# Twenty of the 96 pieces of the experts' weights are split in the state space stage instead of the second cross-attention

## What is computed

```python
x = x + _L0_xattn_ref(_layernorm(x), ctx_1024, ctx_1024, fside, mask, ...)   # cross-attention, 16 heads
x = x + _L0_attn_ref(_layernorm(x), ...)                                    # self-attention
x = x + _L0_ffn_ref(_layernorm(x), ...)                                     # experts, first kind
x = x + _L1_xattn_ref(_layernorm(x), ctx_1024, ...)                         # second cross-attention
x = x + _L1_attn_ref(_layernorm(x), a_params, B_w, C_w, D)                  # state space recurrence
x = x + _L1_ffn_ref(_layernorm(x), ...)                                     # attention with rotation, then top-2 of 8 experts
```

## Time and profile before

| | us |
|---|---|
| median of 3 runs | 1137.86 |
| lowest and highest | 1136.81, 1143.95 |
| profiled execution, its own time | 1140.91 |
| its span (first to last instruction) | 1139.1 |
| PE busy | 839.9 (74%) |
| DVE busy | 586.6 (51%) |
| ACT busy | 447.3 (39%) |
| POOL busy | 398.5 (35%) |
| mean granted clock of TensorE | 0.853 of full |

### The profile page before, as it was taken

The page is one execution under the profiler, slowest core; times in us unless marked ns, Lnnn a source line. Parts: engine busy times, 40 slices in busy tenths (PEclk is TensorE's granted clock), DMA queues, the critical chain, the costliest instruction groups (busy, mean ns, idle before and its releaser), DMA issues.

```text
span 1139.1 us, 23921 instructions
## 1 busy us (share of the span) xinstructions
PE 839.9 (74%) x8324; PEld 662.2 (58%) x8324; DVE 586.6 (51%) x1548; ACT 447.3 (39%) x1619; POOL 398.5 (35%) x577
## 2 busy tenths in 40 slices
PE   2898898689798768888876625675548887788880
PEld 1666666578653346666654514563438786787770
DVE  2477777568644335664563765764314443334342
ACT  1565666356523216655651023664003232222220
POOL 3455655535477742443345323224340000000005
PEclk9999999889889779999995657876559988888885
DMA  7111114523224523243324002111197788886754
GB/s 307 47 47 55 39 53 133 210 76 109 92 99 148 171 98 103 92 139 120 109 77 145 0 1 93 39 38 48 62 328 282 282 291 309 298 301 244 263 211 115
DMA packets 90181, 161.62 MB, mean 142 GB/s; under 512 B 9840, under 2 KB 23920, under 8 KB 89328
## 3 DMA queue, kind: packets, MB, share of 16 engines
q1 hardware_dynamic: 88560, 156.30, 40.1%
q0 software_dynamic: 1536, 4.20, 1.2%
HBM read 126.13 MB, written 34.34 MB: 141 GB/s over the span
## 4 chain that ended last, share of the span: by engine, by line
PE 36%; DMA 15%; DVE 14%; ACT 14%; POOL 9%; issue 9%; SPq 1%; DVEq 0%; POOLq 0%; ACTq 0%
DMA kbuf<-in_b 10%; ACT probs L1094 5%; PE ps L491 4%; PE ps L493 4%; PE ps L492 4%; PE ps L528 3%; ACT probs L1053 3%; PE ps L571 3%; PE ps L587 2%; DMA ctx_t<-in_ctx 2%; PE ps L540 2%; DVE stat L1439 2%; ACT probs L1044 2%; PE ps L620 1%; ACT pt L1033 1%
## 5 line engine op out<-in xcount | busy, mean ns | idle before, releaser
L491 PE MATMUL ps<-qbuf,arena 128*128 128x128 f16 x736 | 149.1, 241 | 46.3 <-DMA kbuf<-in_b 45.7
L492 PE MATMUL ps<-qbuf,arena 128*128 128x128 f16 x736 | 148.9, 241 | 0.0
L493 PE MATMUL ps<-qbuf,arena 128*128 128x128 f16 x736 | 148.4, 240 | 0.0
L1902 DVE SCALAR_TENSOR_TENSOR probs<-ps,kbuf,ctx_t 128x128 f32<-128x128 f32 x184 | 51.8, 344 | 168.9 <-ACT ctx_t L1206 168.9
L1259 POOL TENSOR_TENSOR piece_out<-piece_in,piece_out 128x512 f16<-128x512 f32 x96 | 113.8, 1185 | 7.7
L1422 POOL DMA_INDIRECT pt<-y_rows,neg x16 | 15.4, 960 | 276.0 <-DMA y_rows<-vbuf 271.5
L1206 ACT ACTIVATE ctx_t<-ps,kbuf 128x128 f32<-128x128 f32 x184 | 52.6, 369 | 150.0 <-PE ps L493 150.0
L1227 POOL TENSOR_TENSOR var<-mv,half 128x1 f32<-128x1 f32 x56 | 11.2, 199 | 283.1 <-DVE mv L1440 196.3
L491 PEld LDWEIGHTS ps<-qbuf,arena 128*128 128x128 f16 x736 | 81.0, 110 | 48.6 <-DMA kbuf<-in_b 47.6
L1284 POOL TENSOR_TENSOR probs<-probs,gp 128x512 f32<-128x512 f32 x64 | 81.3, 1302 | 52.4 <-ACT probs L1044 52.4
L571 PE MATMUL ps<-pack_const,probs 128*128 128x128 f32 x512 | 76.5, 285 | 28.8 <-DVE vbuf L1481 11.2
(11 more groups left out here) (231 smaller groups left out, 2003.6 us busy)
## 6 DMA issues: line engine op xcount, KB each, us to landing
arena<-w_parts SPq DMA_DIRECT2D x23, 3072.0 KB, 11.1
piece_in<-in_w SPq DMA_DIRECT2D x96, 256.0 KB, 2.8
w_parts<-piece_out SPq DMA_DIRECT2D x96, 256.0 KB, 2.1
ctx_t<-in_ctx SPq DMA_DIRECT2D x32, 256.0 KB, 2.7
x_rows<-piece_out SPq DMA_DIRECT2D x1, 2944.0 KB, 16.5
qbuf<-x_rows SPq DMA_DIRECT2D x23, 128.0 KB, 9.9
y_rows<-vbuf SPq DMA_DIRECT2D x23, 128.0 KB, 9.7
arena<-in_xa SPq DMA_DIRECT2D x2, 1282.0 KB, 7.0
```

What stands on the lines that cost most here:

```text
L491: pe.matmul(dst, a[0], b[0], start=first, stop=False)
L492: pe.matmul(dst, a[0], b[1], start=False, stop=False)
L493: return pe.matmul(dst, a[1], b[0], start=False, stop=final)
```

## The change

In "xa1" each of the 20 steps splits one piece instead of two, and SyncE passes one piece ahead of each context load. In "ssm" each of the ten steps splits two pieces at its end. The number of splits up to "la" stays 82, and SyncE's loop over the remaining pieces begins earlier.

```diff
         XA1_PIECES = 2 * INNER_STEPS + 2 * (TILES + 1)
-        LA_PIECES = XA1_PIECES + 2 * (SEQS + 4)
+        LA_PIECES = XA1_PIECES + SEQS + 4 + 2 * (TILES + 2)
...
             for k in range(SEQS + 4):
-                pass_piece(XA1_PIECES + 2 * k)
-                pass_piece(XA1_PIECES + 2 * k + 1)
+                pass_piece(XA1_PIECES + k)
                 if k + 2 < SEQS:
                     load_context("xa1", k + 2, k % 2)
-            for c in range(LA_PIECES, EXPERTS * PIECES):
+            for c in range(XA1_PIECES + SEQS + 4, EXPERTS * PIECES):
                 pass_piece(c)
...
                     if st == "xa1":
-                        for j in range(2):
-                            split_piece(j, k + XA1_PIECES // 2)
+                        split_piece(s, h + XA1_PIECES // 2)
                     chain.restart()
...
                     if live(k, 2, TILES):
                         root_of_variance(g, k - 2)
+                    for j in range(2):
+                        split_piece(j, k + (XA1_PIECES + SEQS + 4) // 2)
                     chain.restart()
                 skewed(pool, TILES, 2, ssm_step)
```

## The result

The changed kernel takes 1144.91 us (median of 20 runs, 1141.12 to 1149.09) against 1139.16 (20 runs, 1134.47 to 1146.62) for the kernel before: a ratio of 1.0043 with a 95% interval of 1.0027 to 1.0060. It is slower by an amount inside the 1% that was called no change. Its profiled execution took 1146.38 us with a span of 1144.5, which is 5.4 more than the span before. A ratio is not the quotient of the two medians (that is 1.0050 here). Two slow executions are left out of all numbers: one at 1971.82 us, of the kernel with the pair ahead of the inverse root, and one at 1278.89 us, of the kernel before that ran beside it.

A forecast was written before the change was run, and what follows sets the result against it. It took a circle of engine handoffs (latency, no engine full in the state space stage) to bound the kernel. -5.65 + 1.5 + 4.3 + 7.1 = +7.2 us, 0.63%, scaled from 1137.86 to 1145 us; range 1137 to 1153.

The forecast's parts named there:

- a tile period under 21.5 us: Cross-attention: a period this short would make the forecast wrong; it expected near 21.7 instead of 22.4 us.
- (a): Second cross-attention: context load issued one split sooner, five PE waits go and no more; -5.65 us, between 4.7 and 9.0 gained.
- rival 1: Splits find room in the state space stage and the cross-attention circle follows the load by 1.8 us: -1.7 us, 1136; chance 0.10.
- read, not guessed: Cross-attention: PE's query projection ends at 488.87, leaving a wait of 0.71 us; the reason given for taking 5.65.
- (b): State space stage's start: VectorE's instructions with two SBUF inputs held beside GpSimd; +1.5 us, from 0.3 to 3.
- some four of them meet a bias or split that they didn't meet before: State space stage's start: VectorE instructions newly held, 0.55 us each, less the two that already met one.
- (c): State space stage, five intervals: the pair of splits holds VectorE's phase turns, 0.85 us each; +4.3 us, between 0.5 and 11.
- Both bounds: State space interval: lower, GpSimd's own length, 0.1 us a step; upper, four VectorE instructions losing 0.55 each, 2.2 a step.
- rival 2: VectorE and GpSimd hold each other up fully, 2.2 us a state space step and 3 at the start: +16.4, 1154; chance 0.20.
- (d): State space stage's end: three pairs between sixth inverse root and first rotary one, 14.7 us for 7.6; +7.1, between 6.5 and 8.
- cycles of 5.5 us: State space stage's end: pairs with nothing between, each split waiting for its piece; two such cycles and one pair, 11.0 + 3.7.
- Rival 3: Clock: a longer idle stretch could leave the attention stage's clock lower; 2 us either way, no chance of its own.

The follow-up runs named there:

- the first kernel with reads: Kernel before plus two idle GpSimd casts and subtractions per state space step, no transfers, the last linked to what follows: intervals of 6.7 to 7.1 us.
- one split a step, alone: Kernel before with one split a step in the cross-attention, none in the state space stage, 20 moved to the attention stage: 1135.74 us against 1140.69, ratio 0.9958.
- the kernel that writes: Kernel before plus four GpSimd memsets (128x928) in each state space step, nothing waiting for the last: five intervals 30.3 us; 1149.16 and 1151.24 us for this and its reading counterpart.
- the one that reads without transfers: Kernel before plus two idle GpSimd casts and subtractions per state space step, nothing waiting for the last: five intervals 35.5 us; 1149.16 and 1151.24 us with its writing counterpart.

## Why the prediction was right, and where its terms were off

It said 1145 us with a loss of 0.6%; the median is 1144.91 and the loss 0.43% (0.27 to 0.60). Which way, and that it stays within 1%, was right, and so were the parts that make it. That the microseconds agree to one is partly luck: the sum was +7.2 where the four stretches measure +4.3 and the medians +5.75, and the kernel before ran 1.3 us above the median that I scaled from. One of the prediction's own signs of being wrong came true, too: a tile period under 21.5 us. It is 21.43, because the wait in (a) was larger than I read it; it is not the 1.8 us of rival 1.

**(a) was too small**, 5.65 forecast and 7.3 measured. The mechanism was right: the load is the last input, the wait goes and no more of the 1.8 us. The size of the wait was not. What I took as "read, not guessed", the query projection's end at 488.87, was a modelled end. By the start of the next matmul once nothing was late, PE was ready 0.99 us after 487.71, at 488.70, and the true wait was 0.88, not 0.71. The matmuls behind it then took 1.99 us and not 1.89, 0.1 more. Together 1.0 a tile, in four tiles 4.05 us where the waits that I counted gave 2.96. The tile with the slow landing gave 4.45 us and not 2.69, since the late load cost more than the wait. Granted clock of the stretch ahead and of the one right behind that wait, before (the eighth number of a row):

```profile
501.10:512.00 10.90, 9.22 (x89) 6.62 (x88) 7.70 (x12) 6.45 (x23) 6.39 (x9) 1.00 0.36 119
514.00:518.60 4.60, 4.60 (x41) 3.29 (x41) 0.00 (x0) 1.57 (x6) 1.84 (x3) 0.63 0.43 135
```

and PE's timeline, a tile earlier and behind the wait of 2.69 us:

```profile
491.50 1.08 PE L610 MATMUL ps<-pt,vbuf 128*32 128x128 f32 x32
...
514.00 2.99 PE L528 MATMUL ps<-ctx_t,arena 128*128 128x256 f32 x8 [2.69 <-DMA ctx_t<-in_ctx]
516.92 1.70 PE L610 MATMUL ps<-pt,vbuf 128*32 128x128 f32 x32
```

The same two groups take 1.99 and 1.08 us a tile earlier: behind 2.69 us without matmuls the granted clock was 0.63 for 4.6 us, where it had been 1.00 (1.00 is the level of 2.4 GHz, 0.50 that of 1.2), and 1.6 us went there. The length of the wait alone doesn't decide this. In the kernel before, profiled again, the clock was 0.50 for 3.4 us behind a wait of 1.89 us (466.59 to 470.00); in the first kernel with reads it stayed at 1.00 behind one of 2.07 us, which ended at 472.78:

```profile
472.80:474.80 2.00, 2.00 (x12) 1.51 (x16) 0.00 (x0) 0.00 (x0) 1.81 (x3) 1.00 0.26 98
```

What decides it stays open. Against the gains, the sixth interval was 1.2 longer than before (21.30 for 20.13). The last five microseconds of that interval, before:

```profile
587.00:592.00 5.00, 4.35 (x58) 3.13 (x62) 2.44 (x7) 1.63 (x5) 0.01 (x1) 1.00 0.00 0
```

and after:

```profile
582.00:587.00 5.00, 5.00 (x50) 3.86 (x54) 1.77 (x5) 0.98 (x2) 0.00 (x0) 0.68 0.00 0
```

It fell to 0.68 within the interval in the changed kernel and only behind it in the kernel before (0.50 from 597 to 602). Both values of that interval occur with two splits a step (20.13 and 21.34 in the table) and with one (20.12 and 21.30), so neither needs the change; both profiles with the context load first have 20.12. What decides it stays open.

**(b) was too large**, +1.5 forecast, 0.0 measured. The step that failed is "some four of them meet a bias or split that they didn't meet before". Four are held in the changed kernel, by 0.53, 0.30, 0.10 and 0.30 us, 1.2 in all; but three were held before (0.53, 0.81 and 0.78 us for 0.29), by 1.3 in all. I set two against the new meetings where three went, and my 1.5 is not even what my own numbers give: four less two, at 0.55 each, is 1.1. With no pair in the stage the same start took 20.2 us (one split a step, alone) where before and after had 20.9, so the meetings cost the stretch an estimated 0.7 us in both kernels. VectorE at the stage's start; before, beside the row of 618.64 in the earlier trace rows:

```profile
618.19 0.53 DVE L1782 TENSOR_TENSOR rot<-scratch 128x128 f32<-128x128 f32 x1
...
620.34 0.78 DVE L1782 TENSOR_TENSOR rot<-scratch 128x128 f32<-128x128 f32 x1
```

and after:

```profile
609.07 0.81 DVE L1784 TENSOR_TENSOR rot<-scratch 128x128 f32<-128x128 f32 x1
...
613.76 0.59 DVE L1782 TENSOR_TENSOR rot<-scratch 128x128 f32<-128x128 f32 x1
...
615.44 0.39 DVE L1782 TENSOR_TENSOR rot<-scratch 128x128 f32<-128x128 f32 x1
...
619.97 0.59 DVE L1782 TENSOR_TENSOR rot<-scratch 128x128 f32<-128x128 f32 x1
```

**(c) was right**, +4.3 forecast, +4.8 measured. Laid out in advance were 0.35, 0.25, 0.1 and 0.6 us for the four instructions; the interval shown has 0.18, 0.41, 0.00 and 0.53, 1.1 us for the 1.3 laid out. Normalising gave 0.2 back, where I had counted no loss and 0.1 to 0.3 from the shorter first cast. Both bounds hold as bounds: 0.1 a step is what GpSimd's own length costs (the kernel that writes), and 2.2 a step, rival 2, was not reached. In the interval shown one instruction was held by nearly the 0.55, two by less and one not at all; that this comes from the PSUM readers between them is my reading of the timeline, no run takes them away.

**(d) was right**, +7.1 forecast, +6.8 measured, 6.0 of it by the last two pairs. The forecast's cycles of 5.5 us from the earlier trace rows held: 5.26 us from root to root (662.84 to 668.10) and 5.24 to the rotary one. In the earlier trace rows the waits for a piece were up to 1.17 us, here 0.75 and 0.65. Two cycles shorter by 0.25, less a first pair that took 3.9 us and not 3.7, is the 0.3 of difference.

**The rivals.** Rival 1 needed splits that cost VectorE nothing and a circle that follows the load by 1.8 us. The kernel with the context load first refutes the second half (1.0), the one that reads without transfers the first. Rival 3: over the five intervals the granted clock was 0.75 where it had been 0.73, and 0.50 in the stage's end both times; in one interval of the cross-attention the clock took 1.2 us, and the range held it.

The change does two things that have nothing to do with each other. It frees the context load, worth 7 us, and it moves 20 splits to a place that costs 11.6. The first needs no move at all: with the transfers reordered and all splits left in place the kernel has the lowest median of the study and 0.9940 of the time before. (The one with one split a step and the rest in the attention stage, 0.9958, can't be told from it: the intervals overlap.)

## What to carry to other kernels

When an engine's queue holds an urgent transfer behind work for later, reorder the queue before moving the work; it may be all the gain there is. Idle time of GpSimd is not free room: ask what the other engine's instructions read at that moment, lay the one timeline over the other, and count the meetings that end as well as those that begin. A moved step costs in full where its new stage runs out, so look at the first instruction behind the last copy of it and at who waits for that.

## What the runs showed of the hardware

- A load that lands late can cost more than its wait. Of six profiles with two pieces ahead of the context load in the cross-attention, five had one tile of 23.7 to 25.9 us among those of 22.4; of six with the load first or one piece ahead, none had one over 21.5. Behind waits of 2.69, 1.89 and 1.91 us the granted clock had fallen to 0.50 to 0.63, and the tile lost 1.6 to 1.8 us beyond the wait; behind 2.05 and 2.07 us it stayed at 1.00, and the tile lost little more than the wait (2.3 us against 21.43).
- A row of eight matmuls is drawn over the start of the next by some 0.17 us (1.16 long, next start after 0.99). A wait on PE that is read against the end of the row before is too small by that much.
- GpSimd's memsets, which only write, left VectorE's instructions with two inputs in SBUF at 0.29 us, and held the normalising one (one tile in, scalars beside it) at 0.84 for 0.41.
